# A fused attention and gated-FFN layer on one core: the second element of the first pair takes its softmax maxima one head at a time, and the orders of the fill are laid anew

## The reference

```python
x = layernorm(x + attention(x))   # 16 heads of 8, causal, distance penalty -(i-j) on the scores
x = layernorm(x + ffn(x))         # ffn: h = silu(x w1 s1) * (x w2 s2)
                                  #      h = gelu(h h1 s); h = gelu(h h2 s); return h w3 s
# attention: softmax(q k^T / sqrt(8) + mask + decay) v, then Wo and its bias
# ternary weights in the ffn (512 wide), float32 throughout
```

## Time and profile before

| | us |
|---|---|
| median of 3 runs | 789.07 |
| lowest and highest | 787.79, 789.2 |
| the profiled execution | 788.52 |
| its span (first to last instruction) | 786.8 |
| PE busy | 742.4 (94%) |
| DVE busy | 610.6 (78%) |
| ACT busy | 561.0 (71%) |
| POOL busy | 487.4 (62%) |

### The profile page before, as it was taken

The page is one execution under the profiler, slowest core; times in us unless marked ns, Lnnn a source line. Parts: engine busy times, 40 slices in busy tenths (PEclk is TensorE's granted clock), DMA queues, the critical chain, the costliest instruction groups (busy, mean ns, idle before and its releaser), DMA issues. The chain is left out here.

```text
span 786.8 us, 19041 instructions
## 1 busy us (share of the span) xinstructions
PE 742.4 (94%) x6218; PEld 508.8 (65%) x6218; DVE 610.6 (78%) x2887; ACT 561.0 (71%) x908; POOL 487.4 (62%) x584
## 2 busy tenths in 40 slices
PE   3678999999999999999999999999999999999995
PEld 1455566676767676676767666676767667675763
DVE  3978878787978878797878878797887979787232
ACT  5055858778695967768686877869596776868775
POOL 4164365667575665667576566757656566757764
PEclk8558999999999999999999999999999999999997
DMA  7510302112030301103030211203030120300000
GB/s 215 174 30 5 112 2 83 46 45 85 16 113 2 117 14 60 70 16 114 16 113 2 88 41 50 80 16 114 2 115 15 60 70 3 114 3 30 1 1 29
DMA packets 26540, 44.91 MB, mean 57 GB/s; under 512 B 3240, under 2 KB 6632, under 8 KB 26440
## 3 DMA queue, kind: packets, MB, share of 16 engines
q1 hardware_dynamic: 26440, 43.67, 16.2%
HBM read 12.20 MB, written 4.19 MB: 21 GB/s over the span
## 5 line engine op out<-in xcount | busy, mean ns | idle before, releaser
L949 DVE CUSTOM_DVE_ANT_0 ps<-ps,causal 128x256 f32<-128x256 f32 x960 | 308.3, 389 | 44.4 <-PE ps L610 43.7
L1146 POOL TENSOR_TENSOR hlo<-hf,hhi 128x512 fp32r<-128x512 f32 x128 | 164.1, 1293 | 128.3 <-ACT hhi L883 128.3
L793 ACT ACTIVATE pt<-ps 128x768 f32<-128x768 f32 x256 | 194.7, 807 | 38.9 <-PE ps L648 34.8
L1107 POOL TENSOR_SCALAR_AFFINE_SELECT pt<-pt 128x512 f32<-128x512 f32 x256 | 160.0, 639 | 92.9 <-ACT pt L793 88.8
L873 ACT ACTIVATE hf<-ps,vec_sb 128x512 f32<-128x512 f32 x128 | 88.1, 688 | 111.6 <-PE ps L568 110.2
L562 PE MATMUL ps<-hhi,h_hi 128*128 128x512 f32 x496 | 146.9, 417 | 0.3 <-ACT hhi L883 0.3
L568 PE MATMUL ps<-hlo,h_hi 128*128 128x512 f32 x496 | 134.1, 391 | 0.3 <-POOL hlo L1146 0.3
L949 DVE DVE_READ_ACCUMULATOR2_ANT m<- 128x1 f32 x960 | 131.6, 137 | 0.0
L568 PEld LDWEIGHTS ps<-hlo,h_hi 128*128 128x128 f32 x496 | 93.1, 188 | 23.6 <-POOL hlo L1146 1.2
L665 PE MATMUL ps<-pt,vst 128*32 128x256 f32 (+1 forms) x2048 | 105.6, 337 | 0.3 <-POOL pt L1107 0.3
L562 PEld LDWEIGHTS ps<-hhi,h_hi 128*128 128x128 f32 x496 | 84.1, 188 | 20.2 <-issue 3.0
(11 more groups left out here) (121 smaller groups left out, 1132.7 us busy)
## 6 DMA issues: line engine op xcount, KB each, us to landing
qs<-q_hi SPq DMA_DIRECT2D x30, 256.0 KB
ks<-k_hi SPq DMA_DIRECT2D x30, 256.0 KB
xT<-in_x SPq DMA_DIRECT2D x16, 256.0 KB, 2.7
x_tok<-in_xtok SPq DMA_DIRECT2D x16, 256.0 KB, 2.7
out<-o_tok SPq DMA_DIRECT2D x16, 256.0 KB, 2.0
qs<-q_lo SPq DMA_DIRECT2D x15, 256.0 KB
ks<-k_lo SPq DMA_DIRECT2D x15, 256.0 KB
qs<-no_max SPq DMA_DIRECT2D x15, 64.0 KB
```

The costliest lines, as they stand in the source:

```text
L793: nc.scalar.activation(pt[u][:, c:c + 2, :], ps[:, first:last + 1, 0:3 * P], ACT.Exp).then_inc(t_free.sem, 1)
L949: part = nc.vector.tensor_tensor_reduce(ps[:, bank, cols], ps[:, bank, cols], mask, 1.0, LOWEST, ALU.add, ALU.max, m32[b][:, it, c + e, u: ...
L1107: nc.gpsimd.affine_select(out=diag, in_=diag, compare_op=ALU.is_ge, fill=0.0, base=0, pattern=[[0, 2], [0, 2], [1, P]], channel_multiplier ...
L1146: nc.gpsimd.tensor_tensor(h_lo[layer % 2][:, m, :], hf[:, n % 4, :], h_hi[layer % 2][:, m, :].bitcast(F32), ALU.subtract).then_inc(hlo_rea ...
```

## The change

The second element of pair 0 no longer takes its maxima with `s` and `smax` in the `SCORE` banks. It uses `s1` and `smax1` in the `FB` banks, sixteen steps on each of the two engines in place of eight. The first `st` of pair 0 then has to wait for the first element's maxima alone. The counts of the semaphores are shifted (`wait_max`, `first_max`), and all tables of the fill are written anew. Some steps of the slot and of the drain change places too.

```diff
 PE_FILL = [
     ("qq", 0), ("qk", 0), ("qv", 0), ("qq", 1), ("s", 0, 0, 0), ("s", 0, 1, 0), ("s", 0, 2, 0), ("s", 0, 3, 0),
...
+    ("s", 0, 4, 0), ("s", 0, 5, 0), ("qk", 1), ("s", 0, 6, 0), ("s", 0, 7, 0), ("s1", 1, 0, 0, 0),
+    ("s1", 1, 0, 1, 0), ("qv", 1), ("s1", 1, 1, 0, 0), ("s1", 1, 1, 1, 0), ("s1", 1, 2, 0, 0),
...
+    ("s1", 1, 7, 0, 0), ("s1", 1, 7, 1, 0), ("s1", 0, 0, 0, 1), ("s1", 0, 0, 1, 1), ("s1", 0, 1, 0, 1),
+    ("st", 0, 0, 0), ("s1", 0, 1, 1, 1), ("s1", 0, 2, 0, 1), ("mT", 1, 0), ("s1", 0, 2, 1, 1), ("st", 0, 1, 0),
...
 PE_ORDER = [
...
-    ("g", 0, -1), ("u", 0, -1), ("qk", 1), ("st", 0, 2, 0), ("st", 0, 3, 0), ("pv", 0, 0, 0), ("g", 1, -1),
+    ("u", 0, -1), ("g", 0, -1), ("qk", 1), ("st", 0, 2, 0), ("st", 0, 3, 0), ("pv", 0, 0, 0), ("g", 1, -1),
...
 SP_ORDER = [
-    ("mTd", 0, 0, 0), ("mTd", 0, 1, 0), ("xload", 2), ("qstack", 1), ("mTd", 1, 0, 0), ("tload", 0),
-    ("mTd", 1, 1, 0), ("kstack", 1), ("store", -2),
+    ("tload", 0), ("mTd", 0, 0, 0), ("mTd", 0, 1, 0), ("mTd", 1, 0, 0), ("xload", 2), ("mTd", 1, 1, 0),
+    ("kstack", 1), ("qstack", 1), ("store", -2),
 ]
...
-        def max_pair(q):
-            return max(q - 1, 0)
+        def wait_max(signal, eng, q, k):
+            signal.wait(eng, max(q - 1, 0), k - HP if q else k)
+
+        def first_max(q, b, n, e=0):
+            return 2 * HP * (2 * q + b - 1) + 2 * n + e
...
             elif i < 2:
-                s_free.wait(eng, max_pair(q), 2 * HP - 1 + i)
+                wait_max(s_free, eng, q, (2 * HP if q else HP) - 1 + i)
...
-                            if (b, n, e) == (0, 0, 0):
+                            if (q, n, e) == (0, 0, 0):
+                                pe.wait_ge(half_stacked[1], 16 * 7)
+                            elif (b, n, e) == (0, 0, 0):
                                 stacked.wait(pe, 0)
-                            wait_first_max_bank(pe, 2 * (HP * b + n) + e)
+                            wait_first_max_bank(pe, first_max(q, b, n, e))
...
-                            if q == 1:
-                                pe.wait_ge(s1_free, 2 * HP * (b + 1))
+                            if q == 1 or (q, b) == (0, 1):
+                                pe.wait_ge(s1_free, first_max(q, b, HP))
                             else:
-                                s_free.wait(pe, max_pair(q), HP * (b + 1))
+                                wait_max(s_free, pe, q, HP * (b + 1))
```

## The result

The changed kernel takes 790.98 us (median of 8 runs, 790.13 to 792.12), the kernel before 788.39 (8 runs). The ratio is 1.0031, 95% interval 1.0022 to 1.0039: slower by 0.3%, or 2.6 us between the medians. One run of the kernel before took 2161.72 us and is no part of the ratio. The profiled execution took 790.13 us at a span of 788.4, against 788.52 at 786.8. It is the fastest of the eight, so the traces differ by 1.6 us where the medians differ by 2.6.

A forecast was written before the change was run, and what follows sets the result against it. PE was taken to bound the slots, the chain of dependent steps the fill and drain. Terms +2.8 - 0.3 - 0.6 + 0.3 - 0.6 = +1.6 us on 788.52, plus 0.55 to the median, made 790.7 us; 8-in-10 range 786.8 to 793.0.

The forecast's parts named there:

- Pace of the one-head run: Fill, 32 to 46 us: single banks' refill makes one-head maxima steps take 0.83 us each, where DVE alone would want 0.63.
- First `st` 46.4, second 49.3: Pair 0's first exponential scores in the fill start +0.7 us later than 45.74, the second ones +1.9 in all.
- +2.8: Fill: the third `st` of pair 0's second element comes at about 61.0 us instead of 58.23, the delay in all.
- -0.3 up to the last `pv`: Fill from 58 us: PE's content counts, and one one-head step less up to the last `pv` gives back 0.3 us.
- `atr` and `anorm` -0.6: Fill, last `pv` to `atr`: about 1.5 us instead of 2.07, and `anorm` finds DVE free, 0.6 us back together.
- `w_mx` +0.3: Fill: `w_mx` ahead of three maxima steps brings `x1lo` and `qq` of pair 2 later by 0.3 us.
- rival of the early clock: Fill: denser one-head run brings PE's full clock before 50 us, kernel takes 786.7 us; chance 0.10.
- Tables -0.6: End of the fill: table loads moved behind `attT` into ACT's idle time make the exponentials end earlier, 0.6 us back.
- Slots 0: Slots: the changed orders cost 0 us, bounds -1 and +3.
- The swallowed delay: Rival: later slack in the fill takes up the delay, no change, 789.4 us; chance 0.22.
- The slots' rival: Slots: q stack lands behind its reader or a moved DMA holds the queue, 4.2 us or more, 795; chance 0.08.
- The tables' rival: End of the fill: if ACT holds it, all 2.6 us of loads come back; 787.3 with smaller front delay; chance 0.15.

The follow-up runs named there:

- third bank: Changed kernel with bank `PVB` as a third bank for the first 24 one-head maxima steps: 787.88 us against 788.99 for the kernel before, ratio 0.9983.
- table experiment: Changed kernel with the touch of gelu, and so its two table loads, back among the gates of pair 0: 790.52 us, ratio 1.0023 against the kernel before.
- fill-alone kernel: Changed kernel with the slot and drain orders of the kernel before: 789.86 us against 788.76 for the kernel before, ratio 1.0018.
- slots-alone kernel: Kernel before with the slot and drain orders of the changed kernel: 789.91 us against 788.76 for the kernel before, ratio 1.0014.

## Why the prediction was right, and where its terms were not

The launch came out at 790.98 us where 790.7 was said, inside the range, and slower as forecast. That the number is so near is luck in part. The sum said +1.6 us and the medians give +2.6; the median of three before, 789.07, lay 0.7 above the 788.39 of the eight runs that the result is measured against, which hides most of the difference. The mechanism in the fill held, a one-head run paced by the refill of its banks, but not every term of the sum did.

- **Pace of the one-head run (0.83 us a step, clock 0.50, DVE less busy): right.** Measured 0.83 to 0.88, 0.50, and 13.33 us in place of 13.94; the third bank shows the cause. The 19th step reached DVE at 46.70 us, forecast 46.6.
- **First `st` 46.4, second 49.3: a little late.** 45.93 and 48.64. The term of +0.7 at the first `st` measured 0.19, which is not told from nothing. The delay at the third `st` of the second element was the term "+2.8", at 61.0 us; it measured 1.57, at 59.80. This term of the sum was mis-sized by 1.2: 0.7 of it lies already at the second `st`, and the rest behind it, where I had put each further `st` at 0.93 to 1.0 us and the trace has the third at 49.16, only 0.52 after the second. The first `pv` took 1.51 us at half the clock, near the 1.4 said.
- **-0.3 up to the last `pv`: wrong in sign.** The delay grew there, from 1.57 to 2.17. Up to 62 us the granted clock was 0.50, where before it was 0.86 from 58 to 60 us and full after that, and the second element's work fell into this stretch; the sum had not looked at it. The clock as the cause is read from these rows; no run took it apart. The two errors nearly cancel: last `pv` at 69.39, forecast 69.5.
- **`atr` and `anorm` -0.6.** From the last `pv` to `atr` it is 1.66 us where it was 2.07: 0.4.
- **`w_mx` +0.3: not seen.** From the end of `wo` to `qq` of pair 2 it is 9.12 us (75.78 to 84.90), where it was 9.19 (74.39 to 83.58).
- **What the sum did not have:** the full clock in `wo`, which gives back 0.9 us. The forecast had this only inside the rival of the early clock. In the one-head run the clock stayed at 0.50 and rose only after 62 us, later than before (0.84 against 0.98 from 58 to 72). The Trainium skill (TensorE: Matmul & The Clock Gate, Part 1) has activity release the throttled clock; the denser run of this kernel did not bear that out, while the changed kernel with two extra matmuls did (1.00 from 31 us on).
- **Tables -0.6: mis-sized, about -0.1.** By the table experiment the new place gives 0.1 us from the end of `wo` to the end of the fill. With `w_mx` that stretch became 0.2 us shorter in all (26.11 to 25.90), where the two terms said 0.3. Two loads with the touch between them take from 74.52 to 77.33 us, 2.81. The 1.38 us of drain with a load that the Trainium skill gives (ScalarE: Activation LUTs, What ACT_TABLE_LOAD costs) do not show between these rows: 74.52 + 1.28 is 75.80, and the touch starts at 75.81.
- **The fill in sum**: forecast +1.6 at its end (102), measured 1.18 in the profiles (101.68; 0.7 and 1.5 in two other kernels with this fill) and 1.1 in the timed fill-alone kernel.
- **Slots 0: mis-sized.** The timed slots-alone kernel says 1.1 us (0.4 to 1.8), the slots' length against the kernel before 0.6, and the touch ahead of `exp(1,6)` is worth 0.8 to 0.9 by the traces. The term lies within the stated bounds, -1 to +3, but with it the whole is +2.6 where the sum had +1.6, and that although the fill came out half a microsecond below its forecast. I had gone through the moved PE groups and SP's queue; the 0.18 us instruction that ACT has ahead of the exponential that PE waits for I had passed over, although it is in the order. That a slot would still be 44.9 us long was wrong: it is 45.00.

The rivals. The swallowed delay did not happen: half of the 2.2 us is there at the end of the fill. The early clock did not come (0.50 until 62 us), and forced it cost more. The slots' rival named the q stack behind the k stack; in the trace the last of the four q-stack DMAs of slot 2 is issued from 141.74 to 142.40 us and its reader starts at 146.85. With the 2.0 us that the forecast took for the landing, 2.4 us of cover were left, and that mechanism did not act. The slots do cost a quarter of its 4.2 us, by another. The tables' rival is refuted by the table experiment (0.1 us, not 2.6).

## What to carry to other kernels

Moving work to idle buffers frees the first ones, but the new place has a pace of its own: count the whole circle (fill, drain, and both hand-overs) through one buffer, and if it is longer than the buffers' number times the busiest engine's step, try a third buffer. Here it brought the fill's end 3.7 us forward in the traces, where the one new order of the scores that was tried brought nothing. In a loop of many turns look at the engine that frees what the full engine needs next, and keep even an instruction of 0.18 us from standing ahead of it. When a sum comes out right, take its halves apart before trusting its terms, and look whether the base that it started from has moved. Before reading tenths of a microsecond off two traces, look by how much two executions of the same steps differ: here it was over half a microsecond in the place of the first `st`, but a few hundredths in the length of a slot.

## What the runs showed of the hardware that was not expected

PE was busy for all of the 34 us from 36 to 70 us in the kernel with one extra matmul, and the granted clock stayed at 0.50 throughout; with two extra matmuls, begun with the two-head steps, it was 1.00 from 31 us on at the same full busy share. With two extra matmuls on the kernel before the clock fell back to 0.50 at about 46 us, and PE was busy for 19.41 of the 20 us from 52 to 72 without its rising. So the busy share that the profile shows did not tell whether the clock would rise. What the chip goes by was not settled here.
